# A four-stage graph kernel: the one-head stage on two sets of four PSUM banks, and every stage written out without loops

## The reference, cut to what matters

```python
# layer 0: attention with 8 heads, then a feed-forward network
normed = layernorm(hidden)
logits = q @ k.T / sqrt(32) + (2 * adj - 1)
weights = softmax(logits) * (0.25 + 0.75 * adj);  weights /= weights.sum(-1)
hidden = hidden + (weights @ v) @ Wo + bo
hidden = hidden + gelu(layernorm(hidden) @ Wf1 + bf1) @ Wf2 + bf2
# layer 1: graph attention, once with 8 heads of 32, once with 1 head of 256
h = layernorm(x) @ W                      # per head
e = leaky_relu(s[:, None] + t[None, :], 0.2) + adj;  s = h @ a_src;  t = h @ a_dst
x = x + softmax(e) @ h
```

## Time and profile before

| what | us |
|---|---|
| median of three runs | 1133.56 |
| the profiled execution | 1134.18 |
| its span | 1132.3 |
| PE busy | 1078.1 (95%) |
| DVE busy | 772.2 (68%) |
| ACT busy | 715.3 (63%) |
| POOL busy | 406.3 (36%) |

### The profile page before, as it was taken

One profiled execution on the slowest core, in us unless ns is written; L12 is line 12 of the kernel. 1 busy time (PEld: TensorE's weight loads), 2 busy tenths in 40 slices (PEclk: granted clock), 3 DMA queues, 4 the chain that ended last, 5 costly groups with the idle time before them and its releaser, 6 DMA issues.

```text
span 1132.3 us, 41370 instructions
## 1 busy us (share of the span) xinstructions
PE 1078.1 (95%) x16172; PEld 943.2 (83%) x16172; DVE 772.2 (68%) x1905; ACT 715.3 (63%) x1702; POOL 406.3 (36%) x628
## 2 busy tenths in 40 slices
PE   5999999999999989999999999999999999879897
PEld 5888888888888868899899989998888888767775
DVE  4577776777777767744554455445888988758786
ACT  2777677677677755434553455436778888657673
POOL 3431121211211114321232123222577888675552
PEclk9999999999999999999999999999999999889899
DMA  7001111011100010000000000000000000001112
GB/s 223 30 30 51 37 30 31 30 38 50 30 12 2 3 36 23 1 1 0 0 0 0 0 0 0 0 1 10 22 21 19 27 19 20 4 20 68 62 56 93
DMA packets 41736, 31.18 MB, mean 28 GB/s; under 512 B 5280, under 2 KB 41376, under 8 KB 41632
## 3 DMA queue, kind: packets, MB, share of 16 engines
q1 hardware_dynamic: 37312, 29.36, 8.3%
q10 hardware_dynamic: 4320, 0.28, 0.3%
HBM read 21.25 MB, written 8.39 MB: 26 GB/s over the span
## 4 chain that ended last, share of the span: by engine, by line
PE 82%; DVE 6%; issue 5%; POOL 3%; ACT 2%; ACTq 1%; DVEq 0%; POOLq 0%
PE BK L1381 6%; PE BK L1469 5%; PE BK L1471 5%; PE BK L1470 5%; PE BK L1245 5%; PE BK L1244 5%; PE BK L1243 5%; PE BK L1355 4%; PE BK L1367 4%; PE F L1243 3%; PE F L1245 3%; PE F L1244 3%; PE BK L1348 3%; PE F L1259 3%; PE BK L1533 3%
## 5 line engine op out<-in xcount | busy, mean ns | idle before, releaser
L1097 ACT ACTIVATE gf<-BK,bcol 128x512 f32<-128x512 f32 x128 | 88.2, 689 | 183.1 <-PE BK L1245 169.2
L877 POOL TENSOR_TENSOR ve<-mv,eps_l 128x4 f32<-128x4 f32 x64 | 14.0, 218 | 446.8 <-DVE mv L293 407.9
L1013 ACT ACTIVATE e_sb<-BK,nmx 128x128 f32<-128x128 f32 x512 | 141.8, 404 | 28.3 <-DVE nmx L459 28.3
L1469 PE MATMUL BK<-wf_hi,gh 128*128 128x256 f32 x512 | 143.5, 280 | 0.0
L1470 PE MATMUL BK<-wf_hi,gl 128*128 128x256 f32 x512 | 141.8, 277 | 0.0
L1471 PE MATMUL BK<-wf_lo,gh 128*128 128x256 f32 x512 | 141.7, 277 | 0.0
L550 DVE TENSOR_TENSOR gl<-gf,gh 128x512 fp32r<-128x512 f32 x128 | 93.3, 730 | 63.4 <-ACT gh L1098 61.5
L465 DVE TENSOR_TENSOR pt_sb<-BK,ft 128x512 f32<-128x512 f32 x128 | 85.2, 686 | 69.7 <-PE BK L1355 68.2
L1033 ACT ACTIVATE xn<-x_all,neg_mr,rstd 128x256 f32 (+1 forms) x188 | 103.0, 604 | 6.4 <-POOL neg_mr L886 3.0
L1245 PE MATMUL BK<-xh,wf_lo 128*128 128x512 f32 x256 | 100.9, 394 | 0.0
L1244 PE MATMUL BK<-xl,wf_hi 128*128 128x512 f32 x256 | 100.6, 393 | 0.0
(11 more groups left out here) (206 smaller groups left out, 2880.0 us busy)
## 6 DMA issues: line engine op xcount, KB each, us to landing
x_all<-in_x_dram SPq DMA_DIRECT2D x16, 512.0 KB, 4.3
adj_in<-in_adj_dram SPq DMA_DIRECT2D x32, 256.0 KB, 2.8
out_dram<-y SPq DMA_DIRECT2D x16, 512.0 KB, 2.9
s_wf<-in_L_gnn_Wf_dram SPq DMA_DIRECT2D x2, 1024.0 KB, 10.2
s_w<-in_L_gnn_W_dram SPq DMA_DIRECT2D x2, 256.0 KB, 3.0
s_wq<-in_L_gnn_Wq_dram SPq DMA_DIRECT2D x1, 256.0 KB, 5.2
s_wk<-in_L_gnn_Wk_dram SPq DMA_DIRECT2D x1, 256.0 KB, 6.1
s_wv<-in_L_gnn_Wv_dram SPq DMA_DIRECT2D x1, 256.0 KB, 7.6
```

The source lines that it names most:

```text
L1013: e = act.activation(e_sb[:, j, :], LE[:, r, q, :], ACT.Exp, bias=nmx[:, j:j + 1], scale=1.0)
L1097: act.activation(gf[f % 2][:], BK[:, f % 4, :], ACT.Gelu, bias=bcol[:, 6 + f:7 + f])
L1469: pe.matmul(dst, gh[:, f, n], hi[:, f, :], start=(f == 0), stop=False)
```

## The change

First, `chunks` loses its loop. Each engine's program now holds all 16 chunks of each stage, with constants for wait values and addresses; the two written-out head chunks and the tail stay what they were.

Second, stage D uses all eight banks as two sets of four, by the parity of the chunk. A chunk's projections, turned scores, outer products and the products of `d_av` all lie in its own set. The turned normalised rows of chunk `i + 1` go into the first two banks of chunk `i`'s set, after its projections are copied out and before its outer products (`ln_bank`).

Third, the order in a step of stage D changes on PE, DVE and ACT. `d_outer` of chunk `i - 1` moves behind the second projection of chunk `i`. All four `d_scale` of chunk `i - 1` follow each other behind the statistics. The two low parts stand together ahead of the cap. The third and fourth reciprocal become one instruction. The score columns are copied in two halves.

```diff
@@ -196,14 +193,18 @@
...
-        F = [psum("F0"), psum("F1")]
-        BK = ctx.enter_context(nc.psum_tensor("BK", [P, 6, 512], F32))
+        BK = ctx.enter_context(nc.psum_tensor("BK", [P, 8, 512], F32))
+        F = [BK[:, 6, :], BK[:, 7, :]]
...
-        T_ps = BK[:, 0, 0:2 * P]
-        FC_ps = BK[:, 3, 384:384 + G]
+        T_ps = [BK[:, 4 * r + 2, 0:2 * P] for r in range(2)]
+        FC_ps = [BK[:, 4 * r + 3, 384:384 + G] for r in range(2)]
+
+        def ln_bank(i, par, kt):
+
+            return F[kt] if isinstance(i, int) and i == 1 else BK[:, 4 * (1 - par) + kt, :]
...
@@ -262,14 +263,9 @@
-        def chunks(eng, step, n=NC, tail=2):
-
-            for i in range(2):
-                step(i, 0, i)
-            with eng.Fori(1, (n - tail) // 2) as t:
-                step(t * 2, t, 0)
-                step(t * 2 + 1, t, 1)
-            for i in range(n - tail, n):
+        def chunks(eng, step, n=NC):
+
+            for i in range(n):
                 step(i, i // 2, i % 2)
@@ -651,26 +647,28 @@
...
-            def d_scale(i, g):
+            def d_scale(i, par):
                 dve.wait_ge(d_q, i + 1)
                 dve.wait_ge(d_fc, i + 1)
-                wait_for(dve, d_o, (i - 1) * G + (g + 1))
-                dve.scalar_tensor_tensor(out=pp[0][:, g, :], in0=BK[:, g, 0:P], scalar=f_col[:, g:g + 1], in1=gts(i, g),
-                                         op0=ALU.max, op1=ALU.mult).then_inc(d_pp, 1)
-
-            def d_norm(i, half, par, g):
-                if g == 0:
+                wait_for(dve, d_o, i * G)
+                for g in range(G):
+                    dve.scalar_tensor_tensor(out=pp[0][:, g, :], in0=BK[:, 4 * par + g, 0:P], scalar=f_col[:, g:g + 1], in1=gts(i, g),
+                                             op0=ALU.max, op1=ALU.mult).then_inc(d_pp, 1)
+
+            def d_norms(i, half, par, first, last):
+                if first == 0:
                     dve.wait_ge(y_out[par], half * 16 + Y_START)
-                dve.wait_ge(d_o, i * G + g + 1)
-                dve.reciprocal(crec[:, g, 0:1], BK[:, 4 + g % 2, D:D + 1]).then_inc(d_rec, 1)
-                dve.wait_ge(d_rec, i * G + g + 1)
-                dve.wait_ge(d_xb, i * G + g + 1)
-                dve.scalar_tensor_tensor(out=y_sb[par][:, g, :], in0=BK[:, 4 + g % 2, 0:D], scalar=crec[:, g, 0:1],
-                                         in1=xs(i, g), op0=ALU.mult, op1=ALU.add).then_inc(d_y, 1)
+                dve.wait_ge(d_o, i * G + last + 1)
+                dve.reciprocal(crec[:, first:last + 1, 0:1], BK[:, 4 * par + first:4 * par + last + 1, D:D + 1]).then_inc(d_rec, 1)
+                dve.wait_ge(d_rec, i * 3 + min(first, 2) + 1)
+                for g in range(first, last + 1):
+                    dve.wait_ge(d_xb, i * G + g + 1)
+                    dve.scalar_tensor_tensor(out=y_sb[par][:, g, :], in0=BK[:, 4 * par + g, 0:D], scalar=crec[:, g, 0:1],
+                                             in1=xs(i, g), op0=ALU.mult, op1=ALU.add).then_inc(d_y, 1)
...
@@ -726,39 +724,32 @@
...
                 if ahead:
                     dve.wait_ge(ln_nm, nm_count(i + CD + 1, CD))
-                if back:
-                    d_scale(i - 1, 1)
-                if ahead:
                     dve.wait_ge(ln_st, (i + CD + 3) * G)
-                if back:
-                    d_scale(i - 1, 2)
-                    d_scale(i - 1, 3)
+                if old:
+                    d_norms(*older, 2, 3)
                 if ahead:
                     aggr(i + CD + 2)
-                if old:
-                    d_norm(*older, 2)
-                    d_norm(*older, 3)
                 if far:
                     dve.wait_ge(ln_mv, (i + CD + 3) * G)
                     for g in range(G):
                         stats(i + CD + 3, i + 3, g)
-                d_bias(i)
+                if back:
+                    d_scale(i - 1, 1 - par)
+                d_bias(i, par)
+                if back:
+                    d_norms(*prev, 0, 0)
                 if more and at >= 1:
                     d_lo(i + 1, 1 - par, 0)
+                    d_lo(i + 1, 1 - par, 1)
                 d_cap(i)
                 if back:
-                    d_norm(*prev, 0)
-                    d_norm(*prev, 1)
-                if more and at >= 1:
-                    d_lo(i + 1, 1 - par, 1)
-                d_scale(i, 0)
-            chunks(dve, c2_step, tail=4)
-            for g in range(1, G):
-                d_scale(NC - 1, g)
-            d_norm(NC - 2, NC // 2 - 1, 0, 2)
-            d_norm(NC - 2, NC // 2 - 1, 0, 3)
-            for g in range(G):
-                d_norm(NC - 1, NC // 2 - 1, 1, g)
+                    d_norms(*prev, 1, 1)
+            chunks(dve, c2_step)
+            d_norms(NC - 2, NC // 2 - 1, 0, 2, 3)
+            d_scale(NC - 1, 1)
+            d_norms(NC - 1, NC // 2 - 1, 1, 0, 0)
+            d_norms(NC - 1, NC // 2 - 1, 1, 1, 1)
+            d_norms(NC - 1, NC // 2 - 1, 1, 2, 3)
...
@@ -1161,27 +1152,27 @@
...
                 act.wait_ge(d_h, i * G + g + 1)
-                act.activation(hc[par][:, g, 0:D], BK[:, g, 0:D], ACT.Copy).then_inc(d_hc, 1)
...
-            def d_columns(i):
-                act.wait_ge(d_h, (i + 1) * G)
-                act.activation(sd[:, :, 0:P:32], BK[:, 0:G, D:D + 2].rearrange("p g k -> p k g"), ACT.Copy).then_inc(d_sd, 1)
...
+                act.activation(hc[par][:, g, 0:D], BK[:, 4 * par + g, 0:D], ACT.Copy).then_inc(d_hc, 1)
+
+            def d_columns(i, par, n):
+                act.wait_ge(d_h, i * G + 2 * n + 2)
+                act.activation(sd[:, :, 64 * n:64 * n + 64:32],
+                               BK[:, 4 * par + 2 * n:4 * par + 2 * n + 2, D:D + 2].rearrange("p g k -> p k g"), ACT.Copy).then_inc(d_sd, 1)
...
@@ -1214,26 +1205,27 @@
...
+                if back:
                     normalise(i, CD, (0, 1))
                 d_h_out(i, par, 0)
-                if front:
+                if back:
                     normalise(i, CD, (2,))
                 d_h_out(i, par, 1)
-                if front:
+                d_columns(i, par, 0)
+                if back:
+                    d_f_out(i - 1, 1 - par)
                     normalise(i, CD, (3,))
                 d_h_out(i, par, 2)
-                d_columns(i)
+                d_columns(i, par, 1)
                 d_h_out(i, par, 3)
                 if more:
                     d_hi(i + 1, 1 - par, 0)
-                d_exps(i)
-                if more:
                     d_hi(i + 1, 1 - par, 1)
-                d_f_out(i)
+                d_exps(i, par)
             chunks(act, c2_step)
+            d_f_out(NC - 1, 1)
...
@@ -1594,9 +1586,9 @@
...
-                dst, n = BK[:, g, 0:D + 2], slice(g * P, (g + 1) * P)
+                dst, n = BK[:, 4 * par + g, 0:D + 2], slice(g * P, (g + 1) * P)
                 pe.wait_ge(ln_xh, (i + CD) * KT + KT)
-                wait_for(pe, d_pp, (i - 1) * G + (g + 1))
+                wait_for(pe, d_y, (i - 2) * G + (g + 1))
...
@@ -1605,52 +1597,54 @@
...
-            def d_outer(i):
+            def d_outer(i, par):
 
                 pe.wait_ge(d_cp, i + 1)
                 pe.wait_ge(d_ex, i * 3 + 3)
                 pe.wait_ge(d_hc, i * G + G)
+                if not (isinstance(i, int) and i == NC - 1):
+                    pe.wait_ge(ln_xl, (i + CD + 1) * KT + KT)
                 for g in range(G):
                     row = slice(g * 32, g * 32 + 1)
-                    r = pe.matmul(BK[:, g, 0:P], e_row[row, :], b_row[row, :], start=True, stop=True, tile_position=(g * 32, 0))
+                    r = pe.matmul(BK[:, 4 * par + g, 0:P], e_row[row, :], b_row[row, :], start=True, stop=True, tile_position=(g * 32, 0))
                 r.then_inc(d_q, 1)
-                pe.matmul(FC_ps, f_row[:], ident[:, 0:P:32], start=True, stop=True).then_inc(d_ft, 1)
+                pe.matmul(FC_ps[par], f_row[:], ident[:, 0:P:32], start=True, stop=True).then_inc(d_ft, 1)
...
             def d_av(i, par, g):
                 pe.wait_ge(d_pp, i * G + g + 1)
-
-                wait_for(pe, d_y, i * G + (g - 1))
-                pe.matmul(BK[:, 4 + g % 2, 0:D + 1], pp[0][:, g, :], hc[par][:, g, :], start=True, stop=True).then_inc(d_o, 1)
+                pe.matmul(BK[:, 4 * par + g, 0:D + 1], pp[0][:, g, :], hc[par][:, g, :], start=True, stop=True).then_inc(d_o, 1)
...
-                for g in range(G):
-                    d_h_of(i, par, g)
+                d_h_of(i, par, 0)
+                d_h_of(i, par, 1)
+                if back:
+                    d_outer(i - 1, 1 - par)
+                d_h_of(i, par, 2)
+                d_h_of(i, par, 3)
+                if back:
+                    d_av(i - 1, 1 - par, 0)
+                d_turn(i, par)
                 if more:
-                    d_ln_turn(i + 1, 0)
-                d_turn(i)
-                if more:
-                    d_ln_turn(i + 1, 1)
-                if back:
-                    d_av(i - 1, 1 - par, 0)
```

(19 more changed lines are left out.)

36 lines of the change are left out of this document (16 added, 20 removed).

## The result

The changed kernel took **1125.41 us** in the median of seven runs (1122.72 to 1127.83), beside 1133.69 for seven runs of the kernel before (1130.58 to 1139.03). The forecast was 1125.5. The profiled execution took 1125.41 too; its span, 1123.6, is 8.7 us shorter than before.

What follows compares the result with a forecast made beforehand. PE, busy 95% of the span, bounds the kernel, but DVE's order sets stage D's period. -9.8 - 1.3 + 3 = -8.1 us from the profiled 1134.18 gives 1126.1; that execution being 0.6 above the median, forecast 1125.5, range 1114 to 1137.

Steps and rivals of the forecast that it cites:

- Stages A and B, 0: Stages A and B: bound by PE, busy throughout, so writing out their loops changes 0 us.
- Stage C, +3: Stage C: written-out code makes PE stop for instruction fetches in ten more chunks, losing 3 us, bounds 0 and 19.
- The first chunk, 0 within 2: Start of stage D, hanging on POOL finishing stage C: no change counted, with 2 us either way.
- The period, 7.4: Stage D: period falls from 8.10 to 7.4 us, 9.8 us over 14 periods.
- The saved reciprocal: Stage D, DVE: without loops and with one reciprocal less, four norms take 2.18 us instead of 2.79, saving 0.61.
- the wait ahead of the maximum: Stage D: DVE newly waits about 0.30 us for the score turn, queued on PE behind the first `d_av`.
- the dips gone from the 14 periods: Stage D: two clock dips counted as gone; if they stay, period near 7.6 and gain 7 us.
- not late: Stage D: PE's next projection can start behind the second low part without delaying the period.
- The end, -1.3: Stage D, last outer product to last output: 6.62 us before, 1.3 us saved by the new order.
- DVE without waits: Rival: stage D's period 7.0 us and fetching free in stage C, change -16.7, about 1117 us; chance 0.25.
- Stage C loses more than D gains: Rival: fetch stops in all ten chunks of stage C cost 19 us against 11.1 gained, 1141 us; chance 0.12.
- A wait takes the place of the one removed: Rival: a new PE or `d_scale` wait keeps stage D's period at 8.0 us, about 1134 us; chance 0.15.

Runs made afterwards that it cites:

- e3: Changed kernel with only PE's chunks of stage C back in the old loop: 1121.23 us, ratio 0.9890 against the kernel before.
- e9: Changed kernel with 81 idle semaphore increments ahead of PE's first instruction, shifting all its later code: 1128.99 us, ratio 0.9953 against the kernel before.
- e4: Changed kernel with POOL making chunk 2's deviations and negated mean before finishing stage C's last residual: 1123.41 us, ratio 0.9902 against the kernel before.
- e5: Changed kernel with e3's and e4's edits, and chunk 3's statistics ahead of POOL's first bias addition: 1118.20 us, ratio 0.9859 against the kernel before.
- e7: Changed kernel with stage D's double norm split into two single ones again, four reciprocals a chunk: 1127.76 us, ratio 0.9944 against the kernel before.
- e6: Changed kernel, PE order in stage D: outer products behind the first projection, score turn ahead of the first `d_av`: 1121.98 us, ratio 0.9891 against the kernel before.
- e10: Changed kernel with e5's and e6's edits together: 1112.53 us, ratio 0.9789 against the kernel before.
- e2: Changed kernel with the loops put back on every engine, keeping the new stage D: 1132.26 us, ratio 0.9986 against the kernel before.
- e8: Changed kernel with only DVE looping through chunks 2 to 11 of stage D: 1137.92 us, ratio 1.0020 against the kernel before.
- e12: Changed kernel with only PE looping through chunks 2 to 11 of stage D: 1136.27 us, ratio 1.0002 against the kernel before.
- e13: e12 with POOL's stage D bias additions cut to 4 of 256 columns, a timing-only test: 1122.38 us, ratio 0.9898 against the kernel before.

## Why the prediction held, point by point

- **Stages A and B, 0:** -1.0, within what executions differ by. Held.
- **Stage C, +3:** +7.2 to the last turn of rows and 3.3 regained in the exit, +3.9 in all. The mechanism (fetch behind the small matmuls) is shown by e3 and e9. The size was not right, and that the sum came out near it is luck. First, the stops: only one in the changed kernel is over 1 us (1.48), but there are four more of 0.4 to 0.6, and the clock fell three times between the two marks (801.7, 852.9 and 965.5, 3.4 us each) where one dip was counted, as before. Second, the count of chunks: I took chunks 12 and 13 as written out before, but only DVE's program leaves the loops of stages C and D four chunks before the end; PE's leaves them two before. So the rows held six written-out or first-pass chunks and twelve were to be fetched anew; by the same working (2.57 over six, times twelve) that is 5.1, not 3.2. Third, the exit: the old one had the stop of 1.51 and 10.2 us of low clock, which I hadn't set against it. Fourth, the execution: in the seven later runs with this program on PE in stage C, the stage and its exit cost 6.5 to 9.0 and not 3.9. The old exit's window, and the shorter one after:

```profile
982.60:992.80 10.20, 8.17 (x288) 7.31 (x282) 5.07 (x13) 2.90 (x6) 5.38 (x10) 0.50 0.02 4
```

```profile
989.40:992.80 3.40, 3.40 (x136) 3.14 (x125) 2.43 (x4) 1.10 (x2) 3.40 (x7) 0.50 0.03 7
```

- **The first chunk, 0 within 2:** -0.5 by the maxima. Judged by outer products it looks 3.5 longer, because they moved within the step. POOL's late statistics hold this stretch before as after; e4 and e5 show that they can be moved.
- **The period, 7.4:** 7.35 to 7.38, but for the first (8.54) and the last (7.26). The saved reciprocal, the output 0.19 behind its reciprocal, the wait ahead of the maximum (0.30 predicted, 0.40 found) and the dips gone from the 14 periods all came. **The working was partly wrong**, though: I added up DVE's 6.99 and a wait, and the sum came out at the measured 7.35 since both parts were near (6.95 and 0.40). But the period is the round through PE; e7 shows that work added to DVE's double norm goes into the wait. I also had the projection wait for the last single norm and called PE "not late"; PE waits 0.49 there, and that hand-over is where DVE's half of the round passes to PE.
- **The end, -1.3:** -1.9.
- **The rivals:** "DVE without waits" (7.0) is what e6 and e10 nearly reach (7.06) by another order on PE; the changed kernel lacks it because `d_turn` stands behind `d_av`, as was argued against it. "Stage C loses more than D gains" didn't come, though e9 shows that it depends on the layout: 81 idle instructions cost 3.6 us. Nor was the cost one stop in every chunk, as that rival had it. "A wait takes the place of the one removed", at 8.0, is what happens with a loop on either engine (e2, e8, e12). Its cause in e12, and by the durations a part of it in e2 and e8, are POOL's additions, which I had not seen; the changed kernel meets them too, but where they cost little: its `turn_bias` is free of them and its cap takes 0.35, against 0.22 in e13.

## What to carry to other kernels

Sum an engine's work only to bound a period; then follow the round from engine to engine, since an edit pays only if it lies on that round (e7 lost 0.03 of 0.2, e6 won 0.3 with no work removed). Look at one stage in several executions before you take a difference of a few us in it from two: stage C differed by 3.5 us among eight with the same program on PE. Writing loops out is two edits: decide it by engine and by stage, keep the loop where PE runs through hundreds of small matmuls, and look for "issue" waits that move when the code is shifted. When a tiny operation of DVE takes far longer than elsewhere, look at what POOL does in that moment.

## What the runs showed of the chip that I had not expected

- A run of 128 matmuls of 33 columns stops for up to 2.06 us (e7, at 885.09) with no semaphore, at places that moved by three chunks when 81 instructions were put ahead.
- A loop on PE of two chunks, some 1,460 matmuls and weight loads, runs again with one packet on its fetch queue in 120 us and without a visible cost for the branch.
- A DVE operation of three columns took 0.76 instead of 0.22 us while POOL added 256 columns, and some 12 us of the whole kernel (12.6 by the profiled spans) hung on the length of those additions in e12 and e13.
